# GpSimd weights six of 32 units a chunk in a selective scan, and the prologue's convolution taps go block by block

## The reference

```python
xc, z = split(x @ W_in.T)
xc = silu(causal_conv_4_taps(xc))
dlt, Bm, Cm = split(xc @ W_xproj.T)          # 16, 16, 16 columns
delta = softplus(dlt @ W_dt.T + b_dt)
# for each token, channel d, state n:
h = exp(delta * A[d, n]) * h + delta * Bm[n] * xc
y = sum_n(h * Cm[n]) + xc * D
y = y * silu(z)
```

## Time and profile before

| | us |
|---|---|
| median of 3 runs (5107.31 to 5113.56) | 5111.49 |
| the profiled execution's own time | 5056.72 |
| span of the profiled execution | 5054.9 |
| the Mamba stage in it: first scan to last gate | 61.16 to 1061.96 |
| DVE, PE, ACT, POOL busy over the whole span | 73%, 86%, 56%, 35% |

### The profile page before, as it was taken

The page is one execution under the profiler, slowest core; times in us unless marked ns, Lnnn a source line. Parts: engine busy times, 40 slices in busy tenths (PEclk is TensorE's granted clock), DMA queues, the critical chain, the costliest instruction groups (busy, mean ns, idle before and its releaser), DMA issues. The chain is left out here.

```text
span 5054.9 us, 84397 instructions
## 1 busy us (share of the span) xinstructions
PE 4342.6 (86%) x20410; PEld 3064.2 (61%) x20411; DVE 3700.1 (73%) x7521; ACT 2830.2 (56%) x6544; POOL 1747.8 (35%) x1517
## 2 busy tenths in 40 slices
PE   6887787769999879999999999999976649999960
PEld 2333333336666447888888888888865637777740
DVE  6999999966666678888888888888854433333349
ACT  6777777522222118888888888888843314444420
POOL 5777777620000011122121212122137743333321
PEclk8999999999999989999999999999987869999985
DMA  1000000021111461211121112212135445555558
GB/s 42 13 13 13 13 13 9 9 69 36 36 36 35 151 188 26 52 31 49 27 58 26 50 26 59 51 26 51 34 116 169 164 127 157 156 150 155 156 174 276
DMA packets 329081, 384.68 MB, mean 76 GB/s; under 512 B 124209, under 2 KB 263337, under 8 KB 323003
## 3 DMA queue, kind: packets, MB, share of 16 engines
q1 hardware_dynamic: 255931, 265.05, 17.8%
q0 software_dynamic: 26112, 73.44, 4.1%
q10 hardware_dynamic: 46944, 45.16, 3.3%
HBM read 230.26 MB, written 153.24 MB: 76 GB/s over the span
## 5 line engine op out<-in xcount | busy, mean ns | idle before, releaser
L1539 DVE TENSOR_TENSOR probsT<-ps_t,probsT 128x512 fp32r<-128x512 f32 (+3 forms) x1280 | 779.6, 609 | 137.8 <-ACT probsT L1479 116.2
L1479 ACT ACTIVATE probsT<-ps_t 128x512 fp32r<-128x512 f32 (+3 forms) x1280 | 686.6, 536 | 255.8 <-PE ps_t L1327 231.2
L1471 ACT ACTIVATE probs<-ps_s,negm 128x512 f32<-128x512 f32 (+3 forms) x1297 | 812.4, 627 | 28.1 <-DVE negm L1532 27.1
L1339 PE MATMUL ps_o<-probsT,vbuf 128*128 128x512 f32 (+3 forms) x2560 | 815.8, 402 | 6.8 <-ACT folding L1485 6.2
L1314 PE MATMUL ps_s<-kbuf,qbuf 128*128 (+1 forms) x2602 | 768.7, 380 | 59.2 <-ACT probs L1471 31.5
L1519 DVE TENSOR_REDUCE pmax<-ps_s 128x1 f32<-128x512 f32 (+3 forms) x1301 | 777.6, 600 | 48.6 <-PE ps_s L1314 24.3
L1327 PE MATMUL ps_t<-idn,probs 128*128 128x128 f32 x4352 | 694.8, 275 | 13.8 <-DVE probsT L1539 13.8
L445 POOL TENSOR_TENSOR dBx<-u,b_all 128x1024 f32<-128x1024 f32 x256 | 616.2, 2409 | 237.0 <-DVE h L531 226.3
L1327 PEld LDWEIGHTS ps_t<-idn,probs 128*128 128x128 f32 x4352 | 517.4, 142 | 135.2 <-DVE probsT L1539 41.0
L1314 PEld LDWEIGHTS ps_s<-kbuf,qbuf 128*128 128x128 f32 x2602 | 445.5, 189 | 179.0 <-issue 65.4
L1422 POOL CAST qbuf<-qstage 128x512 fp32r<-128x512 f32 x132 | 81.4, 616 | 1272.1 <-DMA qstage<-q_scr 748.1
(11 more groups left out here) (249 smaller groups left out, 7243.5 us busy)
## 6 DMA issues: line engine op xcount, KB each, us to landing
xr<-xs ACTq DMA_DIRECT2D x294, 136.0 KB
parts<-y SPq DMA_DIRECT2D x36, 1024.0 KB, 5.2
qstage<-q_scr SPq DMA_DIRECT2D x528, 64.0 KB
w_gu<-W_guT SPq DMA_DIRECT2D x64, 384.0 KB, 3.5
q_scr<-rot SPq DMA_DIRECT2D x64, 256.0 KB, 2.9
attn<-ostage SPq DMA_DIRECT2D x128, 128.0 KB, 2.0
at<-attn SPq DMA_DIRECT2D x32, 512.0 KB, 4.1
w_d<-W_downT SPq DMA_DIRECT2D x64, 192.0 KB, 3.7
```

Of the source, the lines that this page charges most:

```text
L1339: last = nc.tensor.matmul(ps_o[:, lo:], vbuf[:, kb, :, :], probsT[:, g % SLOTS, part, lo:], start=kb == 0 and part == 0, stop=kb == BAND * ...
L1471: nc.scalar.activation(probs[:, k, at:at + n, :], ps_s[:, u % RING, 0:n * P], ACT.Exp, bias=negm[:, tile, :], accum_out=sums[:, s, j, c:c ...
L1479: nc.scalar.activation(probsT[:, g % SLOTS, 0, lo:], ps_t[:, t % 2, lo:], ACT.Copy).then_inc(high_t.sem, 1)
L1539: nc.vector.tensor_tensor(probsT[:, g % SLOTS, 1, lo:], ps_t[:, t % 2, lo:], probsT[:, g % SLOTS, 0, lo:].bitcast(F32), ALU.subtract).then ...
```

## The change

In six of the 32 units of each chunk (v = 17, 19, 22, 24, 27, 30) the product h * C is made by GpSimd in place of VectorE. GpSimd's product reads C from SBUF: ScalarE first copies it from `ps_c` into a new SBUF tile `c_sb` (`take_c`), of which there is one. TensorE, in such a unit, waits for that copy before the next `spread_c`, and then for GpSimd's product (`hc_shared`) before `sum_states`. GpSimd's product for unit q - 1 stands in its list ahead of `drive(q + 2)`. The vector engine's scan of unit q waits for the product of unit q - 2, whose `h` buffer it overwrites.

In the prologue, the taps go block by block (all four taps of block 0, then block 1, ...), ScalarE starts `silu_x` for a half when its two blocks are done, and the second `make_delta` of chunk 0 goes behind the first scan.

```diff
+    SHARED_AT = (17, 19, 22, 24, 27, 30)
+        c_sb = sb("c_sb", [P, 1, TC])
+        def shared(q):
+            return q % STEPS in SHARED_AT
+        shared_no = list(itertools.accumulate([int(shared(q)) for q in range(UNITS)]))
...
@@ tensor
-                pe.wait_ge(hc_done.sem, hc_done.at(q))
+                if shared(q):
+                    pe.wait_ge(c_taken.sem, shared_no[q])
+                else:
+                    pe.wait_ge(hc_done.sem, q + 1 - shared_no[q])
                 if q + 1 < UNITS:
                     spread_c(q + 1)
+                if shared(q):
+                    pe.wait_ge(hc_shared.sem, shared_no[q])
                 sum_states(q)
@@ scalar
+            def take_c(q):
+                act.wait_ge(c_ready.sem, c_ready.at(q))
+                if shared_no[q] > 1:
+                    act.wait_ge(hc_shared.sem, shared_no[q] - 1)
+                nc.scalar.activation(c_sb[:, 0, :], ps_c[:, 0, :], ACT.Copy).then_inc(c_taken.sem, 1)
...
-            act.wait_ge(tap_done.sem, DB * TAPS)
             for hv in range(HALVES):
+                act.wait_ge(tap_done.sem, (hv + 1) * DH * TAPS)
                 silu_x(0, hv)
...
                 decay(DH * q + RING)
+                if shared(q):
+                    take_c(q)
@@ gpsimd
+            def weigh(q):
+                pool.wait_ge(c_taken.sem, shared_no[q])
+                pool.wait_ge(scan_done.sem, scan_done.at(q))
+                pool.wait_ge(reduce_done.sem, reduce_done.at(q - 2))
+                nc.gpsimd.tensor_tensor(hc[:, q % 2, :, :], h[:, q % 2, :, :], c_sb[:, :, :].to_broadcast((P, DH, TC)),
+                                        ALU.mult).then_inc(hc_shared.sem, 1)
...
+                if q and shared(q - 1):
+                    weigh(q - 1)
                 if q + 2 < UNITS:
                     drive(q + 2)
@@ vector
-                for t in range(TAPS):
-                    for j in range(DB):
+                for j in range(DB):
+                    for t in range(TAPS):
...
-                            dve.wait_ge(tap_done.sem, (t - 1) * DB + j + 1)
+                            dve.wait_ge(tap_done.sem, j * TAPS + t)
...
+                if q >= 2 and shared(q - 2):
+                    dve.wait_ge(hc_shared.sem, shared_no[q - 2])
+                elif q >= 2 and shared(q - 1):
+                    dve.wait_ge(hc_done.sem, q - 1 - shared_no[q - 2])
...
-            for hv in range(HALVES):
-                make_delta(0, hv)
+            make_delta(0, 0)
             for q in range(UNITS):
...
                 scan(q)
+                if q == 0:
+                    make_delta(0, 1)
...
-                weigh(q)
+                if not shared(q):
+                    weigh(q)
```

More of the change, by code:

```diff
@@ L142, in mamba @@
         hc_done = tally("hc_done")
+        hc_shared = tally("hc_shared")
+        c_taken = tally("c_taken")
         reduce_done = tally("reduce_done")
```

## The result

The changed kernel takes 5123.53 us (median of 9 runs, 5111.53 to 5132.91) against 5107.30 for the kernel before (9 runs, 5103.28 to 5113.56): ratio 1.003, interval 1.0019 to 1.0041. It is slower by 16 us; 5105.3 was forecast, in a range of 5090 to 5120. The forecast was counted from a median of 5111.5 for the kernel before, which is 4 us more than the nine runs give; in differences, 6.2 us of gain were forecast and 16.2 of loss were measured.

The account below looks back on a forecast made before the run. VectorE was taken to set the pace before, with ScalarE, GpSimd and TensorE holding back the gain after: 5.3 + 7.0 + 1.5 = 13.8, less 11.6 plus 4 for the clock, 6.2 us off 5111.5, so 5105.3; range 5090 to 5120.

Parts of the forecast that it names:

- So I take half, 11.6: Gaps ahead of the sums of units 17 and 30: half of the 23 us that clock falls could cost there.
- I count 4 back: Gap at a chunk's start: it shrinks a little, so 4 of at most 10 us of old clock falls vanish.
- the third rival: Sums of units 17 and 30: a fall each time, 23 us lost against 13.8 or 12.9 gained, 5121; chance 16%.
- The gap of 2.44 us without a fall: TensorE before 376.47, kernel before: no fall followed, the next sums took 1.88; evidence for counting only half the falls.
- Sum of unit 17 at t = 6.0: Chunk 2, from scan 17: TensorE sums only after GpSimd's product, at 6.0 us instead of 4.16.
- Low parts at t = 15.0: VectorE's `low_parts` in unit 20, chunk 2, from scan 17: 15.0 us against 15.07 before, leaving a gain of 0.1.
- GpSimd's row of 17 operations from 13.9 to 55.0: Chunk 2, from scan 17: products, drives and one `make_u`, from C of unit 19 to the product of unit 30.
- Seven second halves at full clock +1.5 us in all: Chunks 0 to 6: five middle chunks gain 3.5 us together, chunks 0 and 4 lose about 1 each.
- The last half 7.0: Last chunk, which prepares nothing: six times 1.32 us come through, less 0.35 and some 0.5 of waits.
- The prologue 5.3: Taps block by block: a gain of 5.3 us, taken between bounds of 4.4 and 6.2.
- The kind bound of 6.2: Prologue, if other blocks' taps hide between arrivals: second SiLU ends at 28.0, not 34.27, gaining 6.2 us.
- the 63 us of the second rival: Mamba stage: VectorE stays the bound, 48 moved products give 1.32 us each, 5043; chance 8%, wholly or half.

Follow-up runs that it names:

- second trace: The changed kernel run again unaltered, for its spread and another profile: 5126.35 us against 5105.65 for the kernel before, ratio 1.0041.
- the filled kernel: Changed kernel plus two needless TensorE matmuls before its wait for GpSimd's product in units 17, 22, 24, 27, 30: 5107.65 us against 5115.43 for the kernel before.
- the kernel with four shared units: Changed kernel with products 17 and 19 back on VectorE (22, 24, 27, 30 stay shared): 5078.70 us against 5060.42 for the kernel before, ratio 1.0037.

## Why the prediction was wrong

The step that failed is in the part on the clock: "So I take half, 11.6", and "I count 4 back". The worth of nine falls (14.6 us) was lost in the second halves of the first trace and of fifteen (25.3) in the second, and nothing came back: the clock still fell at the start of each chunk, and the first halves took 2 more. With the sum of the other terms at full clock that turns a gain into the loss of the third rival, "The clock falls in every chunk", which gave 5121 and got 16%. The mechanism was named; its size was not. The gap of 2.44 us without a fall was one gap, with plain sums on either side; ahead of unit 17 stand two gaps with a 0.5 us matmul between. I weighed these by a coin. How long a gap is doesn't settle it either: behind single gaps of 1.9 us the clock stayed up in chunk 6 of the changed kernel, and fell in every middle chunk of the version that defers only unit 17's sum.

The Trainium skill's page TensorE: Matmul & The Clock Gate, section HAM oscillation — how this bites in real kernels, tells of a matmul kernel with waits longer than most gaps here, whose clock falls again at each repetition. The second trace here agrees in the main, with 13 of 14 sums; the first has 8 of 14.

The other terms, against the filled kernel, in whose second halves no shared sum took over 2 us:

- Sum of unit 17 at t = 6.0: 6.03 (6.01 in the changed kernel). Low parts at t = 15.0, scan 21 at 16.87, the saving of two products gone before it: right.
- GpSimd's row of 17 operations from 13.9 to 55.0, 41.1 long: 14.1 to 55.7, so 41.6, measured in chunk 6. Its beginning moves with each fall ahead of unit 17.
- Seven second halves at full clock +1.5 us in all: 444.9 against 444.8, so 0. Middle chunks gain 0.4 on average, not 0.7; chunks 0 and 4 lose 0.9, as said.
- The last half 7.0: 6.5 without falls (53.45), 4.9 and 6.9 in the two traces.
- The prologue 5.3: SiLU's end moved by 5.0. Then TensorE's low clock in the next projections took part of it, and the first gate came 2.7 and 5.7 sooner. Scan 0 started 8.1 sooner, not 5.7, which the gate didn't see. The kind bound of 6.2 was wrong, since the taps of block 1 do lie beside GpSimd's cast:

```profile
17.33 5.34 DVE L536 SCALAR_TENSOR_TENSOR xc<-xraw,taps,xc 128x512 f32<-128x512 f32 x3
...
25.86 2.33 DVE L536 SCALAR_TENSOR_TENSOR xc<-xraw,taps,xc 128x512 f32<-128x512 f32 x3
```

Three such taps take 2.33 alone; beside the cast 5.34. SBUF — State Buffer of the Trainium skill, section Who interferes with whom, says that a VectorE instruction with two SBUF inputs contends with a GpSimd one that reads SBUF; these rows agree.

So 13.8 at full clock was 9.1 (2.6 + 6.5 + 0). Less the 25.3 of the second trace that leaves a loss of 16.2, about what was measured; the first trace is of the fastest of the nine runs and has fewer falls. The prediction also let the 63 us of the second rival go, rightly for the lists as they stood. But it took their order as given, and with the sums one unit later 36 us of gain came.

## What to carry to other kernels

Handing an operation to a slower engine lengthens the time until its result is there, even if that engine has room. In a list that is worked off in order, all that stands behind the consumer waits as well, so the consumer must move back in its own list when the producer becomes slower; here that one move turned 16 us of loss into 36 of gain. Where a change opens gaps ahead of matmuls on the path that sets the end, carry a fall of the clock at each of them as the bad bound with its full weight, and try needless matmuls in the gap to see what the clock costs: here 24 us between the medians (16 over before, 8 under).

## What the runs showed of the hardware

- A fall of TensorE's clock ahead of the two sums that count adds about 1.66 us to the path, whether the gap is one of 3.35 us or two of 1.2 and 1.9. Two needless matmuls in the gap, 1.88 us of work together, prevented it (1.98 for the sum) without a cost that the trace shows.
- GpSimd's product from a copy in SBUF takes 2.35, as its `drive` does, and VectorE's scans beside it are not slowed (2.45 for two). But VectorE's `make_delta`, with both inputs in SBUF, took 2.61 and 3.00 where GpSimd's product or drive had begun ahead of it (the row at 944.34 and that of the kernel with four shared units). Where `make_delta` began first, at 930.58, it took its plain 1.20, and GpSimd's product of 930.80 took 3.18.
- The same instructions between attention and experts take 407 us on one chip and 454 to 469 on two others.
